# Edge pass of a graph layer on one core: node products over three PSUM banks by halves, message sums over two, group steps in another order

## What is computed

```python
h = (x @ W.T).reshape(n, H, D)                      # H = 8 heads, D = 32
h_src, h_dst = h[src], h[dst]
alpha = einsum('ehd,hd->eh', h_src, a_src) + einsum('ehd,hd->eh', h_dst, a_dst)
enc = relu(edge_attr @ edge_W.T + edge_b).reshape(-1, H, D)
alpha = alpha + sum(enc * h_dst, axis=-1)
alpha = where(alpha >= 0, alpha, 0.2 * alpha)
amax = segment_max(alpha, dst)
ex = exp(alpha - amax[dst])
denom = segment_sum(ex, dst)
out = segment_sum(h_src * (ex / max(denom[dst], 1e-10))[..., None], dst)
```

## Time and profile before

| | |
|---|---|
| median of three runs | 5372.19 us (5364.89 to 5379.21) |
| the profiled execution | 5386.62 us, span 5384.8 us |
| PE, DVE, ACT, POOL busy | 72%, 48%, 39%, 38% of the span |
| mean granted clock of PE | 0.843 |
| HBM | 389.57 MB read, 55.13 MB written |

### The profile page before, as it was taken

The page is one execution under the profiler, slowest core; times in us unless marked ns, Lnnn a source line. Parts: engine busy times, 40 slices in busy tenths (PEclk is TensorE's granted clock), DMA queues, the critical chain, the costliest instruction groups (busy, mean ns, idle before and its releaser), DMA issues.

```text
span 5384.8 us, 88907 instructions
## 1 busy us (share of the span) xinstructions
PE 3894.4 (72%) x22054; PEld 2499.9 (46%) x22055; DVE 2587.7 (48%) x6056; ACT 2125.3 (39%) x5703; POOL 2060.0 (38%) x2172
## 2 busy tenths in 40 slices
PE   4778995676776666777676676666667767791999
PEld 3357884343343333333333333333333334580888
DVE  6556553554554455555454554454455546341121
ACT  3212331444444444444444444444444445342322
POOL 4120003454554454454444444444445443005111
PEclk8889998787787788788887887888788878895999
DMA  4610112333333333333333333333333332201110
GB/s 153 213 37 22 35 33 70 83 93 90 92 95 90 91 100 90 92 96 95 93 93 93 91 93 92 97 92 93 95 92 102 96 93 72 103 27 53 34 35 30
DMA packets 352302, 449.27 MB, mean 83 GB/s; under 512 B 170970, under 2 KB 275163, under 8 KB 350456
## 3 DMA queue, kind: packets, MB, share of 16 engines
q0 software_dynamic: 95568, 267.78, 19.0%
q10 hardware_dynamic: 108050, 122.83, 7.4%
q1 hardware_dynamic: 148231, 53.53, 4.1%
HBM read 389.57 MB, written 55.13 MB: 83 GB/s over the span
## 4 chain that ended last, share of the span: by engine, by line
PE 38%; another core or an unknown queue 21%; issue 11%; DVE 9%; ACT 9%; ACTq 7%; DMA 3%; DVEq 2%; POOL 1%; SPq 0%; POOLq 0%
ACT dist L770 5%; PE bank L1040 5%; PE bank L1183 4%; PE bank L1195 4%; PE bank L1061 3%; PE bank L1143 3%; PE bank L1005 3%; PE bank L1014 3%; ACTq L737 3%; PE bank L1099 3%; PE bank L1030 2%; ACTq L735 2%; DVEq L355 2%; DVE msg L1540 1%
## 5 line engine op out<-in xcount | busy, mean ns | idle before, releaser
L514 POOL DMA_INDIRECT al<-h_tab,idx x976 | 1022.8, 1048 | 1110.0 <-issue 1104.5
L752 ACT ACTIVATE enc<-bank,eb 128x512 f32<-128x512 f32 x880 | 556.3, 683 | 1768.5 <-remote 1213.1
L514 POOL DMA_INDIRECT gbuf<-h_tab,idx x784 | 793.4, 1012 | 906.4 <-issue 877.4
L1061 PE MATMUL bank<-prod,hsel 128*32 128x128 f32 x7040 | 351.1, 328 | 1001.4 <-DVE carry L1505 444.8
L1040 PE MATMUL bank<-oneh_t,hbt 125*128 125x512 bf16 x2640 | 865.1, 478 | 6.9 <-issue 3.5
L1061 PEld LDWEIGHTS bank<-prod,hsel 128*32 128x32 f32 x7040 | 200.3, 126 | 1190.2 <-DVE carry L1505 474.9
L1099 PE MATMUL bank<-msg,oneh 128*125 128x264 f32 x2352 | 648.2, 422 | 64.9 <-DVE r L1549 47.2
L1460 DVE SCALAR_TENSOR_TENSOR prod<-enc,adst,bank 128x512 f32<-128x512 f32 x880 | 629.4, 737 | 21.4 <-PE bank L1040 7.1
L770 ACT ACTIVATE dist<-iota_n,dtile 128x125 f32<-128x125 f32 x1760 | 550.8, 384 | 0.5
L1099 PEld LDWEIGHTS bank<-msg,oneh 128*125 128x125 f32 x2352 | 468.0, 207 | 173.1 <-issue 87.2
L1549 DVE TENSOR_TENSOR r<-r,bank 125x264 f32 x440 | 188.1, 428 | 614.7 <-issue 282.4
(11 more groups left out here) (255 smaller groups left out, 5747.7 us busy)
## 6 DMA issues: line engine op xcount, KB each, us to landing
dstb<-dst ACTq DMA_DIRECT2D x440, 125.0 KB
al<-pen_d SPq DMA_DIRECT2D x1760, 4.0 KB
att<-attrx ACTq DMA_DIRECT2D x880, 24.0 KB
al<-h_tab,idx POOLq DMA_INDIRECT x976
link<-links SPq DMA_DIRECT2D x880, 0.2 KB
gbuf<-h_tab,idx POOLq DMA_INDIRECT x784
attrx<-al ACTq DMA_DIRECT2D x8, 1176.0 KB, 12.3
hsplit<-hb POOLq DMA_DIRECT2D x25, 375.0 KB, 6.0
```

Of the source, the lines that this page charges most:

```text
L514: pool.indirect_dma_start(slot(n)[:, c, :], None, h_tab, bass.IndirectOffsetOnAxis(ap=idx[g % 2][:, k:k + 1], axis=0)).then_inc(gathered[n ...
L752: m = act.activation(enc[n % 2][:, k, :], bank[k][:, :], ACT.Relu, bias=eb[:, k:k + 1])
L1061: m = pe.matmul(bank[7][32 * c:32 * c + 32, 0:128], hsel[:, i, :], prod[n % 2][:, k, c * 128:(c + 1) * 128], start=(i == 0 and k == 0), st ...
```

## The change

- `e_dst` takes its PSUM bank by halves: half h = 2n + k goes to bank 2 + h mod 3 (banks 2, 3, 4) in place of four banks for two items. `prod_ready` counts halves, and each half of `e_dst` waits for the product three halves back, so that the second half of item n waits for the first product of item n-1.
- `m_sum` takes banks 5 and 6 in turn and waits for the addition of two items back, not of the last one.
- On PE the group parts stand right behind the head sums of their step. The correction (L1080) moves from `g_up` in step 3 to `g_down` in step 0, and its reader `g_fac` on ACT one step later.
- On ACT `g_x`, `g_exp` and `g_keep` stand right behind `e_relu`, ahead of the loads and the one-hot.
- On DVE `g_scale` and `m_acc` stand behind the products and the group parts, and `e_onehot` and `m_msg` last.

The diff, with less context:

```diff
...
                 act.wait_ge(enc_mm, n + 1)
-                wait(act, prod_ready, n - 1)
+                wait(act, prod_ready, 2 * n - 2)
                 for k in range(KC):
...
             def g_fac(g):
-                act.wait_ge(ends_up, g + 2)
-                act.wait_ge(ends_read, min(g + 2, NG))
+                act.wait_ge(ends_down, g + 2)
+                act.wait_ge(carry_read, min(g + 2, NG))
                 wait(act, acc_scaled, g)
...
                     e_relu(k)
+                if (g := group_at(k, 5)) is not None:
+                    g_x(g)
                 if (g := group_at(k, 9)) is not None:
                     g_exp(g)
+                if (g := group_at(k, 10)) is not None:
+                    g_keep(g)
                 if 0 < k < ITEMS - EB + 1:
...
                     m_oneh(k - 10)
-                if (g := group_at(k, 5)) is not None:
-                    g_x(g)
-                if (g := group_at(k, 10)) is not None:
-                    g_keep(g)
-                if (g := group_at(k, 11)) is not None:
+                if (g := group_at(k, 12)) is not None:
                     g_fac(g)
...
                 pe.wait_ge(node_in, t * 16 + 16)
-                wait(pe, prod_ready, n - 1)
                 for k in range(KC):
+                    wait(pe, prod_ready, 2 * n + k - 2)
                     for a in range(3):
-                        m = pe.matmul(bank[2 + 2 * q + k][:, :], hbt[:, ds(t & (HT - 1), 1), a, k * 128:(k + 1) * 128].rearrange("p t c -> p (t c)"), oneh_t[q][:, :], start=(a == 0), stop=(a == 2))
+                        m = pe.matmul(bank[2 + (2 * n + k) % 3][:, :], hbt[:, ds(t & (HT - 1), 1), a, k * 128:(k + 1) * 128].rearrange("p t c -> p (t c)"), oneh_t[q][:, :], start=(a == 0), stop=(a == 2))
                 m.then_inc(d_ready, 1)
...
                     wait(pe, ends_read, min((k - 8) // G, NG - 1) + 1)
-                    wait(pe, fac_ready, min((k - 8) // G, NG))
                 if k % G == 1:
                     wait(pe, carry_read, min((k - 9) // G, NG - 1) + 1)
+                    wait(pe, fac_ready, min((k - 9) // G, NG))
                 if k % G == 2:
...
                 i = n % G
-                pe.wait_ge(prod_ready, n + 1)
+                pe.wait_ge(prod_ready, 2 * n + 2)
                 for k in range(KC):
...
 
-                if g < NG:
-                    pe.wait_ge(x_local, g + 1)
-                    pe.matmul(bank[7][0:33, A0:A0 + 128], ends[0], ident[:, :], start=False, stop=False, skip_group_check=True)
-                    m = pe.matmul(bank[7][0:33, A0:A0 + 128], ends[1], ident[:, ::-1], start=False, stop=False, skip_group_check=True)
+                pe.wait_ge(x_local, g + 1)
+                pe.matmul(bank[7][0:33, A0:A0 + 128], ends[0], ident[:, :], start=False, stop=False, skip_group_check=True)
+                pe.matmul(bank[7][0:33, A0:A0 + 128], ends[1], ident[:, ::-1], start=False, stop=False, skip_group_check=True).then_inc(ends_up, 1)
+
+            def g_down(g):
+
                 if g > 0:
...
                     m = pe.matmul(bank[7][0:P, B2:B2 + H], oneh[(G * (g - 1)) % NM][0:1, 0, :], dl[0:1, 1, :], start=False, stop=False, skip_group_check=True)
-                m.then_inc(ends_up, 1)
-
-            def g_down(g):
-
-                pe.wait_ge(links_made, g + 1)
-                pe.matmul(bank[7][:, B0:B0 + 2], fin[:, :], ident[0:33, 0:33:32], start=False, stop=False, skip_group_check=True).then_inc(ends_down, 1)
+                if g < NG:
+                    pe.wait_ge(links_made, g + 1)
+                    m = pe.matmul(bank[7][:, B0:B0 + 2], fin[:, :], ident[0:33, 0:33:32], start=False, stop=False, skip_group_check=True)
+                m.then_inc(ends_down, 1)
 
...
                 pe.wait_ge(oneh_ready, n + 1)
-                wait(pe, acc_added, n)
+                wait(pe, acc_added, n - 1)
                 for c in range(4):
-                    m = pe.matmul(bank[6][0:P, 0:HO], oneh[n % NM][:, c, :], msg[n % NM][:, c, :], start=(c == 0), stop=(c == 3))
+                    m = pe.matmul(bank[5 + n % 2][0:P, 0:HO], oneh[n % NM][:, c, :], msg[n % NM][:, c, :], start=(c == 0), stop=(c == 3))
                 m.then_inc(m_used, 1)
...
                     new_sums()
+                if (g := group_at(k, 7)) is not None:
+                    g_up(g)
+                if k % G == 0 and 8 <= k <= G * NG + 8:
+                    g_down((k - 8) // G)
+                if (g := group_at(k, 10)) is not None:
+                    g_turn(g)
                 if k < ITEMS:
...
                     e_dst(k, t[k % EB])
-                if k % G == 3 and 7 <= k <= G * NG + 7:
-                    g_up((k - 7) // G)
-                if (g := group_at(k, 8)) is not None:
-                    g_down(g)
-                if (g := group_at(k, 10)) is not None:
-                    g_turn(g)
                 if 0 <= k - LM - 1 < ITEMS:
...
                     wait(v, r_ready, n - 1)
-                m = v.scalar_tensor_tensor(prod[q][:, k, :], enc[q][:, k, :], adst[:, k:k + 1], bank[2 + 2 * q + k][:, :], ALU.add, ALU.mult)
-                if k == KC - 1:
-                    m.then_inc(prod_ready, 1)
+                m = v.scalar_tensor_tensor(prod[q][:, k, :], enc[q][:, k, :], adst[:, k:k + 1], bank[2 + (2 * n + k) % 3][:, :], ALU.add, ALU.mult)
+                m.then_inc(prod_ready, 1)
 
...
                 v.wait_ge(own_step, known)
-                wait(v, ends_up, g + 1 if g else 0)
+                wait(v, ends_down, g + 1 if g else 0)
                 v.tensor_scalar(dl[0:1, 1, :], dl[0:1, 0, :], -200.0, None, ALU.max).then_inc(dl_ready, 1)
...
                 a = acc[:, ds(t, 1), :].rearrange("p t c -> p (t c)")
-                v.tensor_tensor(a, a, bank[6][0:P, 0:HO], ALU.add).then_inc(acc_added, 1)
+                v.tensor_tensor(a, a, bank[5 + n % 2][0:P, 0:HO], ALU.add).then_inc(acc_added, 1)
 
...
                 g1, g2, g3, g4 = (group_at(k, lag) for lag in (6, 7, 8, LM))
-                if (g := group_at(k, LM + 2)) is not None:
-                    g_scale(g, t_acc[k - LM - 2 - n0])
-                if 0 <= k - LM - 2 < ITEMS:
-                    m_acc(k - LM - 2, t_acc[k - LM - 2 - n0])
                 if g4 is not None:
...
                     g_smax(g1, known)
-                if k + 1 < ITEMS:
-                    e_onehot(k + 1, t_hot[k % G])
-                if 0 <= k - LM < ITEMS:
-                    m_msg(k - LM)
                 if g2 is not None:
...
                     g_smax2(g3, known)
+                if (g := group_at(k, LM + 2)) is not None:
+                    g_scale(g, t_acc[k - LM - 2 - n0])
+                if 0 <= k - LM - 2 < ITEMS:
+                    m_acc(k - LM - 2, t_acc[k - LM - 2 - n0])
+                if k + 1 < ITEMS:
+                    e_onehot(k + 1, t_hot[k % G])
+                if 0 <= k - LM < ITEMS:
+                    m_msg(k - LM)
             v.wait_ge(acc_added, ITEMS)
```

## The result

The changed kernel took 5227.95 us (median of three, 5212.77 to 5252.47) against 5372.19: 0.9729 of the time, 95% interval 0.9703 to 0.9755. Faster, as forecast, with 144 us in place of 252. The profiled execution took 5212.77 us, span 5210.9, clock 0.846. A group now takes 32.1 us (four times the 8.02 us between messages), against 33.6.

What follows compares the result with a forecast made beforehand. The prediction took the edge pass to be bounded by waits, no engine being full. Averaging 5.2 us gained and 0.6 lost gave 2.3 us a group, 253 us over 110 groups: 5120 us, range 4850 to 5450 (forecast alone 5000 to 5300).

Steps and rivals of the forecast that it cites:

- step 3: Loop step with k mod 4 = 3: DVE's ends, chain and fin, 1.64 us, now precede the message, due at +8.9.
- step 0: Loop step with k mod 4 = 0: DVE's carry, scans and difference, 1.52 us, now precede the message, due at +15.0.
- remote: Profile's name for waits without a found releaser; read as PE's completions seen 8 to 9 us late while POOL issues gathers.
- the walk: One group's messages and gathers timed step by step; half the groups in case a, half in case b: 2.3 us gained.
- The wait for L790: PE waiting at the head sums for ACT's copy, 3.3 us a group; should nearly go, about 1.3 us of it free.
- step 1: Loop step with k mod 4 = 1: needs PE's node products, takes 3.6 us; message at +18.6 or +25.8.
- step 2: Loop step with k mod 4 = 2, after the leaky step: message at +4.1, with the 0.42 us addition inside.
- case a: PE seen in or before POOL's gap: gathers go on without pause to +25.8, group 27.2 us, 5.2 less.
- case b: PE seen only after POOL's run ends at +20.8: message at +25.8, next leaky step at +33.0, 0.6 us more.
- the signs that were named: PE's L790 wait below 100 us, POOL gaps below 13.6 us a group, L1549's remote wait moved to L1460 or one-hot, clock about 0.8.
- Rival 3: DVE's group work in steps 3 and 0 holds back POOL, PE's second half waits: 147 us slower, 5520 us; chance 0.20.
- Rival 4: Clock at its lower level, mean below 0.7, makes PE the bound: 5370 to 5480 us; chance 0.06.

Runs made afterwards that it cites:

- b1: The changed kernel, unedited, in a job without late completions: 4218.89 us against 4146.88 for the kernel before, ratio 1.0177.
- the jobs of a, b and d: Follow-up jobs on chips 10, 14 and 5 in which the late completions did not occur; the kernel before took 4143 to 4147 us there.
- d1: The changed kernel with ACT's factor exponential right behind `g_keep`, and two node-tile waits using a register kept at zero or above: 4053.71 us, ratio 0.9769.
- e1: d1 with DVE's leaky step and its two scans behind the message of step 2, with late completions: 5263.54 us against 5435.12, ratio 0.9694.
- e2: d1 with the banks of the kernel before (four node banks, one sum bank), with late completions: 5423.65 us, ratio 0.9977.
- b3: The changed kernel with DVE's addition, one-hot and message ahead of the group work of steps 3 and 0 again: 4221.54 us, ratio 1.0179.
- a4: The changed kernel with four node banks and one sum bank as before, with their waits: 4251.4 us, ratio 1.0252.

## Why the prediction was right, and where it was not

**The bound.** Waits, not an engine: right, and lateness is the largest of them. The two jobs in which it occurs are the longer ones, by 1229 us for the kernel before (5372 against 4143) and 1009 for the changed one (5228 against 4219). All of that lies where gathers are issued: from the first gather to the last the changed kernel took 4055 us after and 3062 in b1, and the rest of the span 1156 and 1152.

The trace also has the semaphore updates themselves, which no row above shows. From 1500 to 3200 us, while POOL was in a run of gathers, a matmul's update followed its shown end by 2.8 us before and 2.4 after (medians of those on record), outside the runs by 0.02; in b1 it followed by 0.02 in the midst of gathers. Updates by DVE and ACT followed by 0.01 in every case. Of 618 updates of the kernel before that came over 2 us late (1500 to 4300 us), 449 came behind the end of a run, the median 1.4 us behind it. So the reading of "remote" was right: it is PE's completions that are late, and the lateness goes with the gathers. It is not shown to be caused by them: in the jobs of a, b and d the same gathers ran nearly without pause and nothing was late, and the kernels without gathers ran only there. The cause stays open.

**Turns behind the head sums, and the walk.** The wait for L790, 293.9 us, went to nothing, as forecast; PE's stand at the head sums fell by 1.9 us a group. The walk can be held against the messages by steps. Its forecast, with half of the groups for each end, was a change of +1.6 us in step 3, -0.1 in step 0, -5.2 in step 1 and +1.4 in step 2, together -2.3. Measured is +4.1, -3.4, -5.2 and +3.0, together -1.5 (times 110, 165 us; the median fell by 144). Step 1 came as forecast on average, though neither of the two ends occurs: POOL never goes on for sixteen gathers (case a), and step 1 takes 5.5 us where case b has 10.8 and case a 3.6. Steps 3 and 0, +0.7 together against +1.5, changed places: DVE no longer stands at the carry copy but at the copy of the ends (L1486). The term that was mis-sized is step 2. Both ends of the walk kept its stall, at +1.4 us on average; with the stalls ahead of it shortened, DVE stands there 10.2 us a group in place of 4.2, and the step grew by 3.0. That the time came within the range owes something to the two ends being averaged half and half. Of the signs that were named, L790 and the clock (0.82) came true; runs longer than twelve or pauses of 1 us did not, and the remote wait of L1549 went over to L1472.

**"The factor's exponential goes one step later, with its reader still behind it: nothing."** Wrong. I looked at its reader on DVE and not at its second follower: `bank7_read` on PE, which waited for it in step 0, now waits for it in step 1, and on ACT it stands 3.5 us behind `e_relu`'s end (2507.47 to 2510.96), behind the loads and the one-hot. b1 measured 3.1 us a group of PE, and d1, which moves that line (and adds the registers), 4.0% between two jobs of like level, 1.5 us a group. In the pair the same wait is there (7.67 us at 2511.22), but beside late completions its removal is worth little: e1 gains at most what its interval allows, and PE waits there at the head sums for L801, which is L790 (367.2 us from 1500 to 4300 us).

**Sums over two banks.** Priced at 0.7 us a group as a wait removed, and counted as hidden. The wait did go. Its larger part is that it lets the addition stand last: without it e2 has 390.9 us of waits in 83 groups, 4.7 us a group. How much of the 2.5 to 2.8% above is this bank's and not the halves' is argued from that line and not shown.

**Node products by halves.** Priced at nothing. PE waits 50.9 us in 57 times, 0.6 us a group or 0.15 a step, under the 0.7 us a step that was named as a sign and the bound of 0.74 + 1.37. It sends PE into its second half late, behind the stall, as the rows at 2523.43 show; no run separates it from the sums' bank.

**DVE's order.** Rival 3 did not decide: b3 moved the message back and changed 1.0177 to 1.0179. That holds where completions are seen at once; with late ones it was not run.

**Rival 4, the clock.** The pass kept 0.82. Where nothing else is late, halves over three banks go with 0.95 against 0.98 for four (b1, a4), and PE's busy time is 861 us against 842. The Trainium skill (TensorE: Matmul & The Clock Gate, A second HAM failure mode: psum-queue depth-cycling) describes a clock that swings between its levels when PSUM banks are cycled. The traces do show one: in these 1000 us the granted clock fell to 0.50 ten times in a4 (34 us in all), 32 times in b1 (109 us) and, with the same three banks but PE no longer idle for L796, 17 times in d1 (92 us). But a4's waits differ too, so that the banks are its cause is not shown.

**The other side.** Slower does occur, by a mechanism that none of my rivals had: where completions come at once the change is 1.8% slower, with 3.1 us a group given away for L796 and no late completions whose stalls could join.

## What to carry to other kernels

When a step is moved, list everyone who waits for its semaphore, on every engine, and put the producer at the head of its engine's step: L796 is 0.16 us long; by its place PE waited 3.1 us a group for it, and another place gave 1.5 of them back. When an extra buffer removes a wait that is short now, price it again for the new order, in which the release may stand last. And a change that is tuned against late completions should be timed where there are none as well; the sign can differ.

## What was not expected of the hardware

The same kernel took 5372 and 5435 us in two jobs and 4143 to 4147 in the others, at granted clocks of 0.843, 0.838 and 0.956. Where completions were late, waits for "remote" were up to 15.0 us long (ACT L763 in e1), a matmul's semaphore followed its shown end by 2.4 to 2.8 us (median, in gather runs of the pair) in place of 0.02, and that of a DVE or ACT instruction by 0.01 as ever. A gather took 1.03 us after and 1.08 to 1.09 in b1 (by line, 1500 to 4300 us), so that the gathers are not themselves slower where PE is.
